# Gated cross-attention and routed FFN on one core: w1 and w3 are split in their own layout and transposed by DMA, batch 1 of the prologue uses other PSUM banks, and the second y maximum goes over TensorE

## The reference, cut to what matters

```python
xn = layernorm(x)                                   # over the 1024
q, k = ws(wq) @ y + bq, ws(wk) @ y + bk             # ws: rows of the weight normalized
v    = ws(wv) @ xn + bv
scores = softmax(q k^T / SCALE)                     # 8 heads, 32 x 32 each
a = norm(ws(wo) @ (scores v) + bo + xn) * gamma + beta
x = x + tanh(g_xattn) * a
t = layernorm(x).reshape(4096, 1024)                # tokens of dimension 1024
gates, idx = top2(softmax(t @ wr.T))
h = silu(silu(t @ w1.T) @ w3.T) @ w2.T              # w1, w3, w2: 1024 x 1024
out[idx[:, k]] += gates[:, k] * h                   # adds to the first 8 token rows only
x = x + tanh(g_ffn) * out
```

## Time and profile before

| what | value |
|---|---|
| median of 3 runs | 1165.01 us (1164.57 to 1166.37) |
| the profiled execution, device time | 1164.77 us |
| its span, first to last instruction | 1163.0 us |
| PE busy, share of the span | 1056.6 us, 91% |
| DVE, ACT, POOL busy | 806.0, 466.8, 415.6 us |
| mean granted TensorE clock | 0.97 of full speed |
| first FFN matmul (L655) starts at | 139.14 us |

### The profile page before, as it was taken

The page is one execution under the profiler, slowest core; times in us unless marked ns, Lnnn a source line. Parts: engine busy times, 40 slices in busy tenths (PEclk is TensorE's granted clock), DMA queues, the critical chain, the costliest instruction groups (busy, mean ns, idle before and its releaser), DMA issues.

```text
span 1163.0 us, 17830 instructions
## 1 busy us (share of the span) xinstructions
PE 1056.6 (91%) x6627; PEld 608.0 (52%) x6627; DVE 806.0 (69%) x1913; ACT 466.8 (40%) x714; POOL 415.6 (36%) x500
## 2 busy tenths in 40 slices
PE   4566279899999999999999999999999999999998
PEld 2355145564556555564556555655556455654452
DVE  6787457896679747986689657975788658973221
ACT  4456333345242633354243533353234524262331
POOL 2472002481147403671158212750167114730000
PEclk9778589999999999999999999999999999999999
DMA  8801700017100540027001620035001700054000
GB/s 269 219 19 55 216 1 1 1 63 188 42 1 27 135 128 0 18 78 192 0 0 36 172 80 0 18 117 153 0 0 72 213 4 0 0 142 149 1 1 2
DMA packets 102753, 81.82 MB, mean 70 GB/s; under 512 B 69342, under 2 KB 87332, under 8 KB 102716
## 3 DMA queue, kind: packets, MB, share of 16 engines
q1 hardware_dynamic: 100656, 79.77, 23.5%
q10 hardware_dynamic: 2060, 1.58, 0.5%
HBM read 47.75 MB, written 16.81 MB: 56 GB/s over the span
## 4 chain that ended last, share of the span: by engine, by line
PE 55%; DVE 23%; POOL 8%; issue 8%; ACT 5%; DMA 1%; ACTq 1%; POOLq 0%; DVEq 0%
PE bank L655 38%; PE bank L531 7%; DVE ub L1206 6%; DVE ub L1225 3%; DVE ub L1221 2%; PE bank L542 2%; POOL xbuf L394 2%; POOL mtmp L391 2%; POOL coc L355 2%; DVE bst L1161 2%; PE bank L554 1%; DVE bst L1216 1%; ACT h_hi L900 1%; DVE act_t L1318 1%; DVE x_hi L1172 1%
## 5 line engine op out<-in xcount | busy, mean ns | idle before, releaser
L655 PE MATMUL bank<-xt_hi,w1b 128*128 128x512 f16 x1024 | 326.7, 381 | 0.0
L655 PE MATMUL bank<-w3b,h_hi 128*128 128x512 f16 x1024 | 304.5, 379 | 0.5 <-DVE act_t L1318 0.5
L655 PE MATMUL bank<-xt_lo,w1b 128*128 128x512 f16 x512 | 194.9, 381 | 0.0
L655 PE MATMUL bank<-w3b,h_lo 128*128 128x512 f16 x512 | 194.0, 379 | 0.0
L894 ACT ACTIVATE act_t<-bank,fs 128x512 f32<-128x512 f32 x128 | 87.1, 680 | 193.8 <-PE bank L655 193.7
L1323 DVE SCALAR_TENSOR_TENSOR h_lo<-act_t,h_hi 128x512 f16<-128x512 f32 x128 | 98.4, 769 | 91.7 <-ACT h_hi L900 91.7
L900 ACT ACTIVATE h_hi<-act_t 128x512 f16<-128x512 f32 x128 | 80.8, 632 | 199.2 <-DVE act_t L1318 199.2
L655 PEld LDWEIGHTS bank<-xt_hi,w1b 128*128 128x128 f16 x1024 | 100.6, 98 | 114.3 <-issue 2.1
L1318 DVE SCALAR_TENSOR_TENSOR act_t<-act_t,bank 128x512 f32<-128x512 f32 x128 | 86.2, 673 | 102.0 <-ACT act_t L894 101.8
L655 PEld LDWEIGHTS bank<-w3b,h_hi 128*128 128x128 f16 x1024 | 98.0, 98 | 76.6 <-DVE act_t L1318 0.5
L410 POOL TENSOR_TENSOR ub<-bo_b,mcur 128x512 f32<-128x512 f32 x64 | 64.6, 1039 | 163.8 <-DVE dg L1183 163.8
(11 more groups left out here) (200 smaller groups left out, 1814.6 us busy)
## 6 DMA issues: line engine op xcount, KB each, us to landing
xbuf<-in_x_dram SPq DMA_DIRECT2D x16, 1024.0 KB, 8.6
out_dram<-xbuf SPq DMA_DIRECT2D x16, 1024.0 KB, 4.2
x_lo<-in_ctx_dram SPq DMA_DIRECT2D x16, 512.0 KB, 3.5
mrow<-in_mask_dram SPq DMA_DIRECT2D x16, 512.0 KB, 4.3
w1b<-in_w_dram SPq DMA_DIRECT2D x8, 512.0 KB, 7.3
w3b<-in_w_dram SPq DMA_DIRECT2D x8, 512.0 KB, 7.7
xbuf<-in_w_dram SPq DMA_DIRECT2D x1, 4096.0 KB, 13.6
xt_hi<-x_hi SPq DMA_TRANSPOSE x32, 4.1
```

The lines of the kernel that those rows point to most:

```text
L655: mm = pe.matmul(bk[:, :], left, right, start=d == 0 and n == 0, stop=d == FT - 1 and n == 2)
```

## The change

The weights are split where they lie, in their DRAM layout, and the f16 halves are transposed by DMA.

- w1 is loaded by row blocks (128 rows, 4 KB each), w3 as before by column blocks. There are 16 blocks of 128 x 1024: i = 0..7 of w1, 8..15 of w3. For each, ACT writes the hi half (`w_high(i)`) from the f32 block in SBUF, DVE the lo half (`w_low(i)`), and SP issues two DMA_TRANSPOSE (`turn(i)`) that put them where the f32 block stood. PE's 128 f32 transposes of `weight` are gone.
- The halves wait for their transposes in five slots, which lie in `h1` and `h2` (the FFN's own outputs): `w_slot(i)` gives a block's slot and how often that slot was used before. Blocks 0 to 4 are split in the prologue, the others at the start of groups 0 to 6 of pair 0 (`w_blocks`). ACT waits for a slot's earlier transposes (`w_turned`) before it writes into it, and before `ffn(0, g)` writes into the part of `h1` or `h2` that a slot used.
- `ffn(0, g)` needs row block g of w1 only; group 8 needs all of w3.
- In the prologue batch 1 is projected into `att[0]`, `att[1]`, `fbk[1]` and `rbk`, its scores and later products use `fbk[1]` and `rbk`, and the first four `long_product` steps of batch 0 come ahead of `times_value` of batch 1. The layer norm of batch 0 (`ln1`) comes later on DVE, and POOL's steps stand in another order.
- The y maximum of pair 1 goes over TensorE (`y_columns(1)`, `y_spread(1)`, inside `ffn(0, 0)`), and POOL's `y_largest(1)` is gone; those of pairs 2 to 7 stay on POOL.
- `tokens_high` writes the f16 tokens straight from x by one ACT instruction for each half of the channels, in turn with the f32 ones; `tokens_low` and the transposes follow by halves. This holds for all pairs.
- The router of pair 0 runs after group 1, as in all pairs.

```diff
+    def w_slot(i):
+        return ((3, 0), (4, 0), (0, 0), (1, 0), (2, 0), (0, 1), (1, 1), (2, 1),
+                (0, 2), (1, 2), (2, 2), (0, 3), (1, 3), (2, 3), (0, 4), (0, 5))[i]
+    def w_blocks(g):
+        return {0: (5, 6, 7), 1: (8, 9), 2: (10, 11), 3: (12, 13), 4: (14,), 6: (15,)}.get(g, ())
...
+        w_part = [[h[:, at].rearrange("p a n -> p (a n)")
+                   for h, at in ((h2, slice(0, 2)), (h1, slice(4, 6)), (h1, slice(6, 8)), (h1, slice(0, 2)), (h1, slice(2, 4)))]
+                  for h1, h2 in ((h1_hi, h2_hi), (h1_lo, h2_lo))]
...
+            def turn(i):
+                slot, used = w_slot(i)
+                sp.wait_ge(sm["w_lo"], i + 1)
+                for part, w in zip(w_part, (w1_hi, w1_lo) if i < FT else (w3_hi, w3_lo)):
+                    sp.dma_start(w[:, i % FT, :].rearrange("c (f p) -> c f p", f=FT), part[slot], transpose=True)\
+                        .then_inc(w_turned[slot], 16)
...
                 load_x(j)
+                if j == 1:
+                    for i in range(FT, 2 * FT):
+                        turn(i)
...
+            for b in range(2):
+                tokens(0, b)
+                turn(b)
             store(0)
-            tokens(0)
+            for i in range(2, FT):
+                turn(i)
...
-            def weight(i):
...
-                for r in range(4):
-                    last = pe.transpose(bk[:, P * r:P * r + P], src[:, n // 2, 4 * (n % 2) + r, :], ident[:, :])
-                last.then_inc(sm["w_tr"], 1)
...
+                    if d == 0 and first_pair(j):
+                        slot, used = w_slot(g)
+                        pe.wait_ge(w_turned[slot], 32 * (used + 1))
+                    f = slice(P * d, P * d + P)
+                    parts = ((w1_hi[:, g, f], xt_hi[:, d, :]), (w1_hi[:, g, f], xt_lo[:, d, :]),
+                             (w1_lo[:, g, f], xt_hi[:, d, :]))
...
+            def w_high(i):
+                slot, used = w_slot(i)
+                if i % FT == 0:
+                    act.wait_ge(sm["w_scale"], 2 + i // FT)
+                need(act, w_turned[slot], 32 * used)
+                src = w1n[:, i, :] if i < FT else w3n[:, i - FT].rearrange("p f c -> p (f c)")
+                act.activation(w_part[0][slot], src, ACT.Copy, scale=sc[:, i // FT, 2:3]).then_inc(sm["w_hi"], 1)
...
                 if w3:
+                    for i in w_blocks(g):
+                        w_high(i)
+                    if g in (0, 2, 4, 6, FT):
+                        n = (0, 2, 4, 6, FT).index(g)
+                        act.wait_ge(w_turned[(3, 4, 1, 2, 0)[n]], (32, 32, 128, 128, 192)[n])
...
+            y_columns(1)
+            pe.wait_ge(sm["wr_lo"], 1)
+            for d in range(FT):
+                if d == 2:
+                    y_spread(1)
+                    w_columns(2)
+                if d == 5:
+                    w_spread(2)
+                ffn(0, 0, d)
```

More of the change, by code:

```diff
@@ L525, in project @@
                     need(pe, sm["x2_ready"], 4 * q - 3 + t)
+                elif bk is not att:
+                    if t < 2:
+                        pe.wait_ge(sm["qk_evac"], t + 1)
                 elif t == 2:
@@ L530, in project @@
                     for left, right in ((y_hi, wqk_hi), (y_hi, wqk_lo), (y_lo, wqk_hi)):
-                        mm = pe.matmul(att[t][:, :], left[b][:, c, P * t:P * t + P], right[:, c, :],
+                        mm = pe.matmul(bk[t][:, :], left[b][:, c, P * t:P * t + P], right[:, c, :],
                                        start=n == 0, stop=n == 5)
@@ L649, in ffn @@
                         pe.wait_ge(sm["h_lo"], GROUPS * j + d + 1)
+                    if g == FT and d == 0 and first_pair(j):
+                        for slot, n in enumerate((6, 4, 4)):
+                            pe.wait_ge(w_turned[slot], 32 * n)
                     k, f = (g - FT) // 2, slice(TOK * (g % 2), TOK * (g % 2) + TOK)
@@ L692, in value_out, with group @@
                 mm.then_inc(sm["w2_tr"], 1)
-            def group(j, g, ja=None, w3=False):
+            def group(j, g, ja=None):
                 for d in range(FT):
-                    if w3 and d in (0, FT // 2):
-                        for i in w3_banks(g, d > 0):
-                            weight(i)
                     if ja is not None:
@@ L865, in tokens_high @@
             def tokens_high(q, b):
-                normed(q, b, co2, sm["ln2_coef"], sm["xs2_ready"])
-                act.wait_ge(sm["xs2_ready"], q + 1)
-                act.activation(tok_hi[b], xs[b], ACT.Copy).then_inc(sm["tok_hi_set"], 1)
+                act.wait_ge(sm["ln2_coef"], q + 1)
+                for c in range(CH):
+                    for x, done in ((tok_hi, "tok_hi_set"), (xs, "xs2_ready")):
+                        act.activation(x[b][:, c, :], xa[b][:, c, :], ACT.Identity, bias=co2[:, 3, c:c + 1],
+                                       scale=co2[:, 2, c:c + 1]).then_inc(sm[done], 1)
             def attention(j, s):
@@ L907, in group @@
             def group(j, g, ja=None, w3=False, jn=None):
-                if w3:
-                    for i in w3_banks(g):
-                        weight(i)
                 if ja is not None and g > 0:
@@ L913, in group @@
                 if w3:
-                    for i in w3_banks(g, middle=True):
-                        weight(i)
-                if w3 and g == FT:
-                    act.wait_ge(sm["fs_set"], 2)
+                    for i in w_blocks(g):
[3 more added lines that the diff above has]
+                        act.wait_ge(w_turned[(3, 4, 1, 2, 0)[n]], (32, 32, 128, 128, 192)[n])
+                    if g == FT:
+                        act.wait_ge(sm["fs_set"], 2)
                 ffn(j, g)
@@ L1436, in _ @@
+            y_low(0, 1)
+            small_largest()
+            below_largest(0, 0)
+            biases()
+            v_low()
+            block_weights(0, 0)
+            w_row(0)
+            dve.wait_ge(sm["ws_copy"], 3)
+            for t in range(CT):
+                qk_out(1, 1, t, bk=(att[0], att[1], fbk[1], rbk))
+            ln1(0, 0)
+            t1_low(0)
+            small_scale()
             small_low()
-            t1_low(0)
             ln1(0, 1)
+            below_largest(1, 1, bk=fbk[1])
```

375 lines of the change are left out of this document (169 added, 206 removed).

## The result

The changed kernel takes 1136.6 us (median of 4 runs, 1136.05 to 1137.7), the kernel before, beside it on the same chip, 1164.9; the ratio is 0.9756, 95% interval 0.9739 to 0.9773. The profiled execution takes 1137.7 us where that of before took 1164.77: 27.1 us less, where 23.7 were forecast. It is the slowest of the four (the spans of the others are 1134.2 to 1135.1 us, its own is 1135.8); by the ratio the change is worth 28.4 us.

The account below looks back on a forecast made before the run. PE bounds the body; a chain of waits bounds the prologue. 1164.77 - 41.3 (35.3 from group 1 forward, 6.0 of PE work) + 17.6 of queue costs = 1141.1, forecast 1141 us; range 1134 to 1150, chance 0.50.

Parts of the forecast that it names:

- Group 1 forward (-35.3): Prologue: the second group of FFN matmuls of pair 0 starts at 121.8 in place of 157.06 us.
- Second norm (1.5): Prologue, between the residual's end at 98.9 and ACT's last tokens at 100.4: the step takes 1.5 us.
- Transposes at 1.37 us: SP's queue: each DMA transpose takes 1.37 us back to back, 256 KB at 191 GB/s.
- a cheaper queue: Rival: contiguous blocks transpose faster, at 0.9 us, or pass the stores; 1125 to 1134 us, chance 0.23.
- one at 2.2 us throughout: Rival: mixed stores, loads and transposes make each transpose cost up to 2.2 us; 1150 to 1161 us, chance 0.19.
- one that waits for each landing: Rival: each weight transpose waits until the one before lands, 3.3 in place of 1.37 us; 1187 us, chance 0.05.
- w3's transposes off PE (-6.0): Groups 1 to 6 of pair 0: six rows of eight f32 transposes, about 1.0 us each, leave PE.
- What the queue costs (+17.6): Pair 0: late DMA transposes hold up ACT and DVE, so PE's new waits and slow clock add 17.6 us.
- the second hold-up: Pair 0: `w_high(11)` waits for w3's block 0, queued behind masks and 2 MB of x, landing at 154.3 us.
- The five waits: PE in pair 0: new waits of 1.6, 3.3, 1.2, 5.0 and 4.5 us for groups, scores and `times_value`.
- The all-reduce: Prologue: POOL's step for the next y's maximum sits 8.78 us; that leaves, as two small matmuls replace it.
- No cost in the body: All pairs: tokens in halves cost ACT 4.8 in place of 4.3 us, adding nothing since PE is 97% busy.

## Why the prediction was right, point by point

**Group 1 forward (-35.3).** Measured -34.3. The mis-sized term is the first: POOL's first `x_low` was left at 47.1 and starts at 48.87, after a wait for ACT. Each step that was named comes later by about as much: coefs of batch 1 at 90.6 in place of 88, `v_normed` at 90.9 in place of 89, the residual's end at 100.9 in place of 98.9, the queue's start at 102.0 in place of 100.1, the first FFN matmul at 115.08 in place of 113.0. But POOL doesn't carry that delay alone. Its coefs of batch 1 wait 0.48 us for DVE's statistics at 87.81, and ACT comes to `v_normed` of batch 1 straight from its row sums, without a gap, 0.3 us after the coefs. The three engines are close to one another there: with the old banks DVE's statistics came 5.9 us later and the first FFN matmul with them, with POOL's old order it came 2.3 us later. That POOL without gaps *is* the gain was too simple. Against the late start stands group 0, which took 7.7 us where 8.8 were counted, so 1.0 of the 2.1 us is left.

**Second norm (1.5).** It took 4.2 us, 100.97 to 105.15. Its first three steps took 1.06, 1.06 and 1.62 us while DVE ran its steps of two SBUF inputs (100.81 to 104.3); batch 0's second and third, with no such step beside them, took 0.19 and 0.70. The Trainium skill, "SBUF — State Buffer", section "SBUF: two separate sides", says that a step with two SBUF inputs and one of GpSimd that reads SBUF exclude each other for a whole instruction; the trace agrees, and with the split behind the tokens the third step is back at 0.70. The miss cost nothing that shows: the queue behind was full anyway, as the prediction said of it, and with 0.8 us of it taken back the token transposes stayed where they were.

**Transposes at 1.37 us.** Measured 1.31 to 1.34 for single weight blocks and 1.36 back to back. The destination makes no difference in these rows: weight blocks land contiguously, tokens in pieces with gaps, and 256 KB in 1.31 to 1.36 us is 193 to 200 GB/s for both. The Trainium skill, "DMA: Bandwidth & Descriptors", section "Latency and other measured facts", has 261 GB/s for a transpose with a middle dimension that is not contiguous and about 350 to 400 GB/s for the contiguous case; it doesn't say that the destination is meant. Both figures are above what these rows show. The rivals of a cheaper queue, of one at 2.2 us throughout and of one that waits for each landing fall with these rows.

**w3's transposes off PE (-6.0).** They are gone from PE; no run prices them alone. The trace of the kernel before makes it 5.2: the rows overlap what follows, and behind each of the six the next matmul starts 0.87 or 0.88 us later, as in this row and in the one at 196.94 in the earlier trace rows.

```profile
196.06 1.04 PE L517 MATMUL bank<-ident,w3b 128*128 128x128 f32 x8
```

**What the queue costs (+17.6).** Measured 12.4, from -27.1 + 34.3 + 5.2 (13.2 with the 6.0 of the prediction). The mechanism, both places and the engines were right: the bank that group 2 needs is free at 135.4 as forecast, the scores go at 140.26 (140.0), and ACT waits ahead of `w_high(5..7)` and `w_high(11)`. The mis-sized term is the second hold-up: masks, 2 MB of x and block 0 were counted at 13.8 us and took 11.35 (139.53 to 150.88), so the second scores start at 162.55 in place of 163.7. Behind them DVE does the gates beside the scores, and `times_value` starts at 171.85 in place of 174.9. That is 3.0 of the 3.4 us by which the total was too high.

The five waits themselves were not met. Up to `times_value` 15.6 us of waiting were counted, and the four rows of PE's timeline show 0.61 + 3.32 + 2.04 + 0.86 = 6.8. In place of waiting PE worked at a low clock (granted 0.50 and 0.54): the two rows of scores took 3.78 and 3.53 us, where they take 1.95 at full clock, and the FFN matmuls behind the first lost about 1 us more. So PE came to group 4 near 159, 2.8 us later than forecast, and found its bank free since 156.2. The prediction said that the next wait swallows the slow clock; that held, and it is why the starts fit better than the waits: the chain through queue, ACT and DVE sets them.

What the sum doesn't show is that taking one hold-up away doesn't give back its waits. While the second stands, it sets the time alone: without the first nothing was gained, without the second 3.2 us of span (2.6 by the ratios), without both 5.5 (4.1, the kernel with the stores behind w3's block 0), and DVE stands close behind.

**The all-reduce.** "The all-reduce's 8.78 us leave with it" fits the old program, where the all-reduce stands in the chain of group 1 and runs only at 146.30; no run takes it out of that program alone. In the new one the same all-reduce costs nothing that can be measured, so no gain from the way over TensorE is shown.

**No cost in the body.** The rows show none: PE is busy 684.1 of 700 us, before 682.9.

**Three readings.** From 120 to 160 us ACT was busy 17.3 of 40 us, a little more than its share in the body (283 of 700), not less; DVE and POOL were less busy, and the argument doesn't hang on it. The 4.1 us of the first 12 FFN matmuls are not all at half clock: from 141.7 on they follow one another at 0.22 us, so "some 4 us" at 1.2 GHz reads too much into them. And cutting the outer half of both neighbours would leave 1129.5 to 1155.5, with 0.71 by the chances given, not 1127 to 1156 with 0.8.

## What to carry to other kernels

A transpose by DMA moves work off PE into a queue in program order: price what stands in that queue ahead of each piece, above all bulk stores and loads, and put those where the queue is idle or where nobody waits. Remove one wait and see whether a later one pays it back before adding up waits: here the first hold-up was free as long as the second stood, and the second was worth 3 us. An edit's worth is that in the new program: undone by itself, one of three parts cost 4.3 us of span, one 0.8 and one nothing, and what they are worth together was not run.

## What the runs showed of the hardware

- After a wait of 3.32 us PE ran the scores at half clock: 16 matmuls took 3.78 us. The first row is of the changed kernel, the second of the one with the stores behind w3's block 0, where PE did not wait and took 1.95 us (granted clock third from the right):

```profile
140.30:144.00 3.70, 3.70 (x17) 3.62 (x18) 2.72 (x3) 2.56 (x3) 0.00 (x0) 0.50 0.93 257
```

```profile
136.40:138.30 1.90, 1.90 (x18) 1.87 (x17) 1.35 (x2) 1.90 (x3) 0.00 (x0) 1.00 0.11 22
```

  The granted 0.50 is 1.2 GHz, 1.00 is 2.4 GHz. So a wait of 3.3 us cost some 5 by the end of the scores. The length of the wait alone doesn't decide it: ahead of the second scores PE waited 2.04 us in the changed kernel and ran them at a granted 0.54 (3.53 us); with the maximum on POOL it waited 2.55 us and ran them at 1.00 (2.05 us, the row below). What does decide it is not shown.

```profile
161.29 2.05 PE L549 MATMUL bank<-ub 128*128 128x128 f32 x16 [2.55 <-ACT ub L841]
```

- A pair of transposes behind 2 MB of stores or loads on the same queue took 7.9 and 8.2 us in place of 2.7; behind one load of 1 MB, in the kernel with the stores ahead of the tokens, it took 4.6. Whether it waits for the queue's order or for the DMA engines was not separated.
